# Third attention: output bias as a three-row 16-bit pass, epsilon of the mixed tiles on ScalarE

## What is computed

```
x = x + tanh(g_ffn[1])   * _L1_ffn_ref(_layernorm(x), ...)          # routed experts
x = x + tanh(g_xattn[2]) * _L2_xattn_ref(_layernorm(x), ctx, ctx, W_q, b_q, ..., W_o, b_o)
x = x + tanh(g_ffn[2])   * _L2_ffn_ref(_layernorm(x), w_fc, b_fc, w_proj, b_proj)

def _layernorm(x, axis=-1, eps=1e-05):
    m = jnp.mean(x, axis=axis, keepdims=True)
    v = jnp.var(x, axis=axis, keepdims=True)
    return (x - m) / jnp.sqrt(v + eps)

_L2_xattn_ref:  softmax(q k^T / sqrt(8)) v @ W_o + b_o
```

## Time and profile before

| | |
|---|---|
| three runs | 1034.47, 1032.77, 1032.52 us, median 1032.77 |
| the profiled execution | 1032.29 us, its span 1030.5 us |
| mean granted TensorE clock | 0.959 of full |
| busy: TensorE, its weight loads | 904.9 us (88%), 695.3 us (67%) |
| busy: VectorE, ScalarE, GpSimd | 839.5 (81%), 676.6 (66%), 576.4 (56%) |
| third attention | about 532 to 692 us |

### The profile page before, as it was taken

How to read it: one execution, slowest core, us unless ns; L and a number is a source line. 1 busy time by engine, 2 the same in 40 slices (tenths; PEclk the granted TensorE clock), 3 DMA queues, 4 the chain that set the end, 5 groups by cost and what they waited for, 6 DMA issues and landing times. The chain is left out here.

```text
span 1030.5 us, 30109 instructions
## 1 busy us (share of the span) xinstructions
PE 904.9 (88%) x11572; PEld 695.3 (67%) x11593; DVE 839.5 (81%) x2240; ACT 676.6 (66%) x1740; POOL 576.4 (56%) x736
## 2 busy tenths in 40 slices
PE   8999999999999980499958999997888999968775
PEld 5888879988888860266636888874446777733332
DVE  6999987878899984356647999987997899978987
ACT  5888874357877750154436777887876788856653
POOL 6444401343347867422248888714665478768884
PEclk9999999999999995799989999998999999979998
DMA  8680000000000011356411111000000000000000
GB/s 224 136 314 2 3 2 2 2 2 2 3 10 28 28 35 49 102 158 183 139 41 34 32 33 31 25 3 1 2 2 1 3 2 3 3 1 16 21 22 26
DMA packets 60527, 44.44 MB, mean 43 GB/s; under 512 B 15196, under 2 KB 55781, under 8 KB 59366
## 3 DMA queue, kind: packets, MB, share of 16 engines
q1 hardware_dynamic: 55718, 34.09, 11.3%
q0 software_dynamic: 4096, 8.34, 2.7%
q10 hardware_dynamic: 576, 0.13, 0.1%
HBM read 23.73 MB, written 18.87 MB: 41 GB/s over the span
## 5 line engine op out<-in xcount | busy, mean ns | idle before, releaser
L2110 DVE TENSOR_REDUCE rowmax<-ps 128x16 f32<-128x1024 f32 x128 | 155.4, 1214 | 27.2 <-PE ps L729 26.3
L1136 ACT ACTIVATE pr<-ps 128x512 f32<-128x512 f32 x256 | 138.8, 594 | 45.2 <-PE ps L798 41.6
L2116 DVE TENSOR_TENSOR sm<-ps,rowmax 128x512 f32<-128x512 f32 x256 | 164.9, 686 | 3.4
L798 PE MATMUL ps<-cst,sm 128*128 128x128 f32 x1024 | 141.1, 277 | 11.6 <-DVE sm L2116 9.6
L756 PE MATMUL ps<-vbd,pr 128*64 128x18 f32 x4096 | 141.8, 212 | 0.6 <-ACT pr L1136 0.5
L756 PEld LDWEIGHTS ps<-vbd,pr 128*64 128x64 f32 x4096 | 134.1, 138 | 5.2 <-ACT pr L1136 1.6
L798 PEld LDWEIGHTS ps<-cst,sm 128*128 128x128 f32 x1024 | 112.0, 141 | 27.7 <-issue 18.6
L1526 POOL TENSOR_SCALAR xn<-x_sb,mv_all,rstd_all 128x128 f32<-128x128 f32 x122 | 98.0, 804 | 35.6 <-PE ps L693 28.3
L1016 ACT ACTIVATE qbd<-ps,bqp,cst 128x128 f32<-128x128 f32 x256 | 104.5, 463 | 5.9 <-PE ps L709 2.0
L1313 POOL DMA_INDIRECT big<-expert_out,row_g x64 | 68.6, 1072 | 40.6 <-DMA expert_out<-xn_all 22.9
L1330 POOL DMA_INDIRECT slots<-xn_all,row_s x64 | 64.7, 1012 | 30.8 <-DVE sm L2116 15.9
(11 more groups left out here) (322 smaller groups left out, 2323.2 us busy)
## 6 DMA issues: line engine op xcount, KB each, us to landing
slots<-hT SPq DMA_DIRECT2D x8, 1024.0 KB, 12.0
sm<-slots SPq DMA_DIRECT2D x32, 256.0 KB, 3.2
expert_out<-xn_all SPq DMA_DIRECT2D x16, 256.0 KB, 2.9
ew<-in_L_ffn_w SPq DMA_DIRECT2D x24, 128.0 KB, 2.6
out<-x_sb SPq DMA_DIRECT2D x32, 64.0 KB, 1.5
slots<-xn_all,row_s POOLq DMA_INDIRECT x64
big<-expert_out,row_g POOLq DMA_INDIRECT x64
x_sb<-in_x SPq DMA_DIRECT2D x1, 512.0 KB, 4.6
```

Of the source, the lines that this page charges most:

```text
L798: last = nc.tensor.transpose(turned[b][:, r * P:(r + 1) * P], sm[x][:, c:c + P], ident)
L1136: nc.scalar.activation(pr[y][:, b, :], turned[b], ACT.Exp, scale=SCALE).then_inc(p_ready[y], 1)
L2110: v.tensor_reduce(row3, sc, AX.X, ALU.max).then_inc(rowmax_ready[x], 1)
L2116: v.tensor_tensor(sm[x][:, :].rearrange("p (r g k) -> p r g k", r=RG, k=S)[:, part], sc[:, part], row3[:, part].unsqueeze(3).broadcast_to( ...
```

## The change

The output bias of the third attention joins bias3 as 128 further columns, and its pass becomes a 16-bit product of three rows. For the mixed tiles from 3 on, VectorE aggregates straight into mv_all, and ScalarE adds epsilon to the variance, as the last instruction of its half-step. Tiles 0 to 2 keep mixed_eps.

```
-        brow = sb("brow", [3, F2 + D])
-        brow_h = sb("brow_h", [3, F2 + D], BF16)
-        brow_m = sb("brow_m", [3, F2 + D], BF16)
-        brow_l = sb("brow_l", [3, F2 + D], BF16)
-        bias3 = sb("bias3", [3, F2 + D], BF16)
+        brow = sb("brow", [3, F2 + 2 * D])
+        brow_h = sb("brow_h", [3, F2 + 2 * D], BF16)
+        brow_m = sb("brow_m", [3, F2 + 2 * D], BF16)
+        brow_l = sb("brow_l", [3, F2 + 2 * D], BF16)
+        bias3 = sb("bias3", [3, F2 + 2 * D], BF16)
...
                         if l == 2:
-                            last = nc.tensor.matmul(mixed[:, M_Y], ident, y_bias_b[2][:, :], start=False, stop=True)
+                            last = nc.tensor.matmul(mixed[:, M_Y], ones_b[0:3, :], bias3[:, F2 + D:F2 + 2 * D], start=False, stop=True)
                         last.then_inc(y_ready[x], 1)
...
+                    blend = mixed_first(t) if l == 2 else None
+                    if blend is not None:
+                        var = mv_all[:, 2 * blend + 1:2 * blend + 2]
+                        act.wait_ge(early_aggr[x], EARLY + blend // NS + 1)
+                        nc.scalar.activation(var, var, ACT.Identity, bias=eps2[:, 1:2], scale=1.0).then_inc(early_eps[x], 1)
...
                     if blend is not None:
                         dve.wait_ge(early_bst[x], EARLY + i + 1)
-                        v.bn_aggr(mv[y][:, :], bst[x][:, :]).then_inc(early_aggr[x], 1)
+                        v.bn_aggr(mv_all[:, 2 * blend:2 * blend + 2], bst[x][:, :]).then_inc(early_aggr[x], 1)
...
-                    if blend is not None:
-                        mixed_eps(x, i)
...
                 elif n == 13:
+                    then(v.tensor_copy(brow[:, F2 + D:F2 + 2 * D], y_bias_b[2][0:3, :]))
                     then(v.tensor_copy(brow_h[:, :], brow[:, :]))
```

## The result

| | before | after |
|---|---|---|
| runs | 1033.72 us median (1032.52 to 1034.77, 7 runs) | 1038.28 us median (1036.47 to 1040.44, 7 runs) |
| ratio | | 1.0041, 95% interval 1.003 to 1.0051 |
| profiled execution's span | 1030.5 us | 1037.8 us |
| mean granted TensorE clock | 0.959 | 0.952 |

Slower: the ratio of the runs gives 4.2 us (0.0041 x 1033.7), the medians differ by 4.6.

What follows compares the result with a forecast made beforehand. Four engines need 4.0 to 4.3 us a half-step, mean 4.47, with starts tied to GpSimd's second gather. +0.2 - 0.5 + 3.7 = +3.4 on 1032.29 gives 1035.7, plus 0.5 for the median: 1036.2; range 1029.5 to 1038.5.

Steps and rivals of the forecast that it cites:

- Preparation: VectorE steps ahead of the expert output copies, widened from 640 to 768 columns: nothing to +0.5 us, +0.2 taken.
- The bias pass: TensorE, third attention: one 16-bit pass for two 32-bit ones, 0.14 us less a half-step, 0.5 us off the tail.
- the rival in the list (chance 0.10): 16-bit pass not cheaper: TensorE stays at 4.30 us, nothing gained in the tail, 1033.0 us without a tie; chance 0.10.
- Epsilon off VectorE: VectorE's 0.15 us epsilon lies in the wait between row maximum and subtraction: gives back 0 to 0.11 us, nothing taken.
- Epsilon on ScalarE: End of ScalarE's half-step: 0.30 us long, 0.19 of ScalarE's time, just fitting the 0.27 us to spare.
- GpSimd: Deviation 0.76 us later behind epsilon, second gather about 0.5 later; with the tie +2.7 to +4.7 us, +3.7 taken.
- the four late ones: Third-attention half-steps, two after each four-tile deviation on GpSimd; forecast at about 5.1 us each.
- The loop: Chain through TensorE, ScalarE's epsilon, GpSimd's deviation and gathers, the tie and the exponential: 9.18 us over two half-steps, 4.59 each.
- The tie: Third attention: reciprocal and exponential start 0.6 to 0.7 us behind the second gather's end, cause unnamed; chance 0.47.
- the rival without a tie: GpSimd's delay is harmless, VectorE paces: quiet half-steps fall from 4.36 to 4.26 us, -2.1 us, 1030.7; chance 0.30.

Runs made afterwards that it cites:

- after_again: The changed kernel, unchanged, timed again beside the kernel before in another session: ratio 1.0002 (0.9991 to 1.0012).
- bias_only: The kernel before with only the three-row 16-bit bias pass and its preparation, epsilon staying on VectorE: 1029.54 us, ratio 0.999.
- A: Follow-up session on one chip, including the bias part alone and the epsilon part alone; the kernel before took 1029.54 us there.
- B: Follow-up session on a second chip, including both kernels repeated unchanged; the kernel before took 1029.70 us there.
- before_again: The kernel before, unchanged, profiled and timed again in session B: ratio 1.0004 (0.9991 to 1.0018).
- after_deferred: The changed kernel with GpSimd's four-tile deviations taken out of the half-steps and issued at t = T - 4: 1034.91 us, ratio 1.0019.
- session C: Follow-up session on a third chip, including the changed kernel repeated and GpSimd's four-tile deviations deferred; the kernel before took 1033.05 us there.

## Why the prediction came out as it did

Forecast +3.4 us, measured +4.2, by the mechanism forecast, but with one term of the wrong sign and with a condition that I did not know. In absolute time it was 1036.2 forecast and 1038.28 measured; 0.95 of the difference is the base, which over seven runs is 1033.72 and not 1032.77. Luck helped twice. The range of 1029.5 to 1038.5 reaches over both signs: it holds the result by 0.2 us, and it would also have held the 1029.58 us of after_again, where the change costs nothing. And the pair was measured in one of the two sessions that have the hold.

1. **Preparation: +0.2 taken, about +0.06 measured.** The last copy starts at 522.93 for 522.29; but the copy ahead of the widened steps is already late by 0.58 (509.62 for 509.04). What is left is 0.06, and the 0.17 us of wait is gone, as foreseen. The 0.58 arose earlier, where nothing was changed.

2. **The bias pass: -0.14 a half-step and -0.5 in the tail taken; +0.08 and +0.3 measured.** This is the step that failed, the term with the wrong sign. It costed the 16-bit pass by eight of them in a row. Here it stands alone between 32-bit matmuls. From the start of L770 to that of the second transpose of L798 TensorE took 0.325 + 0.224 + 0.109 = 0.66 us before (L770 to L772, to L798, to its second) and 0.42 + 0.16 + 0.17 = 0.74 in bias_only: 0.1 more ahead of the pass, and the first transpose behind it holds the next one up by 0.06. One pass less saved 0.07 by itself and the two places where it meets the 32-bit matmuls gave back 0.15. It isn't the three rows: in the kernel before L883 is a pass of the same shape between 16-bit ones, and the next pass starts 0.05 us behind it.
```profile
707.84 0.21 PE L883 MATMUL ps<-bias,ones_b 3*128 3x128 bf16 x1
707.89 0.37 PE L662 MATMUL ps<-bias,ones_b 3*128 3x512 bf16 x1
```
The tail, where TensorE is alone, shows it bare: 4.38 for 4.29. I had the rival in the list (chance 0.10) with no cost beyond lost gain; it is dearer than that.

3. **Epsilon off VectorE: nothing, as taken.** From row maximum to subtraction passes 1.22 us after (612.50 to 613.72) and 1.22 before.

4. **Epsilon on ScalarE: 0.30 us, as estimated**, issued 0.68 behind the key projection (610.10 to 610.78), with 0.70 taken. It paces nothing where nothing is held: the ordinary half-steps of after_again are 4.37 long, as those of bias_only are without it. It has used up the exponential's wait (from 550 to 672 us 6.1 us in bias_only, 0.2 in after_again), but ScalarE still waits 0.3 us a half-step for TensorE ahead of L1073. With the hold the exponential came 1.30 behind the key projection (610.10 to 611.40) and not the 0.95 that I had named as the most.

5. **GpSimd: right in kind and nearly in size.** L1324 starts 0.44 us late, the second gather ends 0.23 behind the start of the mix (0.5 forecast), and the half-steps are (102.64 - 20.73) / 18 = 4.55 in the eighteen ordinary ones (4.59 forecast) and 5.18 in the four late ones (about 5.1). The loop can be read in the kernel after term by term; in its ordinary laps it is 2.61 + 0.99 + 0.76 + 0.98 + 2.45 + 0.65 + 0.65 = 9.09 for the 9.18 of the forecast (gathers together, tie and way to L693 last). So the 22 half-steps cost +4.3 for +3.7, inside the bounds. The sum had no term for the 0.9 us that the first half-steps of the stage lost as well.

6. **The tie is real, and it is a held semaphore.** In the kernel after the release lies 0.31 to 0.57 us behind the second gather whether the deviation starts at once behind that gather or GpSimd idles until after the release (gather ends at 577.31, release at 577.88, L1324 at 578.13), and in the late half-steps too, so it is the gather and not what follows it. The Trainium skill (SBUF — State Buffer, Who interferes with whom) says that TensorE and ScalarE wait on nobody at SBUF; I let that speak for the rival without a tie. The trace doesn't contradict it: what came late was a semaphore, not an operand, and the page's rule says nothing of those.

7. **What the prediction lacked: the hold belongs to the chip or its session.** In A and B the rival "no tie" is true, but its gain of 2.1 us isn't there: the change is level with before (1.0002), although its half-steps are 4.375 and not 4.29. The reading that fits is that GpSimd paces both in the mean: free-running it needs 4.14 us from one second gather to the next (580.73, 584.87, 589.01 in bias_only), plus 1.02 twice in eight half-steps, 4.40 on average, so most of TensorE's 0.08 is hidden, and the mix falls into one wait for gathered rows instead (1.24 us in before_again, 1.11 in after_again). In the two profiles of B the 26 half-steps with gathers take 113.6 and 114.3 us, 4.37 and 4.40 each: 0.7 us more for the change, where 26 times 0.083 would be 2.2. These are single executions, and no run of A or B takes the extra work from GpSimd, so this is argued and not shown. That GpSimd's mean is the largest of the four could have been read from the earlier trace rows; I compared only quiet half-steps with each other and so took GpSimd's 4.12 to lie under TensorE and VectorE. (With the 1.04 that stands in that sum its terms give 4.19; the 4.12 takes 0.97 for it, as the loop does.)

8. **The rest of the profile's 7.3 us**: 0.58 ahead of the preparation and 1.2 behind the stage were not forecast and not tried; the mean clock was 0.952 for 0.959. (In the forecast's reading of before, the four late half-steps are 19.8 us together by the exponentials and not 19.6; its 4.36 for the ordinary ones stands.)

What stays open: what holds TensorE's semaphores while gathers are issued, why it goes with these gathers and hardly with the other indirect DMAs, and why in two sessions of four; and how the 0.19 of after_deferred divides, since the bias part and the epsilon part alone were timed only where nothing is held.

## What to carry to other kernels

Take each engine's own time as a mean over the whole pattern, with what it does only every few half-steps, and not from a quiet one: GpSimd's 1.02 us twice in eight made its mean, 4.40, the largest of the four. Moving that work to where it idles took 0.19% off in session C; that session has the hold, and how much it gives without one wasn't timed. A short 16-bit pass set between 32-bit ones on TensorE isn't priced by such passes in a row; price it from the start before to the start behind. And where an engine starts late though its inputs are long done, look at when the semaphore was raised, and repeat the pair on another chip before building on it.

## What was not expected of the hardware

- The semaphore of TensorE behind L756 went up 0.8 to 2.3 us late while GpSimd issued two indirect DMAs of 1.0 to 1.15 us each; the release came 0.2 to 0.6 us behind the end of the second, but for two half-steps. With some 17 matmuls recorded behind the held one, TensorE also stopped in the middle of L729 for 0.2 us, where nothing is waited for (599.01 to 599.24 in the late half-step of before). All this in two sessions of four, in which the kernel before takes 1033.05 and 1033.72 us; in the others it takes 1029.54 and 1029.70.
- One 16-bit matmul of 3 rows and 128 columns between 32-bit ones takes 0.30 us of TensorE's time, two 32-bit passes of 128 rows 0.22 (both at the full granted clock). Between 16-bit passes the next one starts 0.05 us behind the same matmul.
